# Expert tiles without a bias product: the bias as the 128th weight row, and first-layer weights copied from SBUF

## The chip, the cores and the metric

The program runs on one core of a Trainium2 chip. Its time is the device time in microseconds (us) of one execution; the kernel before has a median of 607.71 us over three runs. Engines are named as the profile names them: PE (TensorE, its matmuls), PEld (its weight loads), DVE (VectorE), ACT (ScalarE), POOL (GpSimd) and SP (SyncE, which only issues transfers here). SPq and ACTq are the transfer instructions on SP and ACT. Sixteen DMA engines carry all transfers, whoever issues them.

## The reference, cut to what matters

Four sequences of 512 tokens of 128 numbers go through attention (16 heads), an expert layer, a scan layer, and the same expert layer again, each on a layer norm of its input and added to it:

```python
x = x + attn_a(layernorm(x)); x = x + ffn(layernorm(x)); x = x + attn_b(layernorm(x)); x = x + ffn(layernorm(x))

def ffn(xf):                       # xf [2048, 128]; 8 experts, each token goes to the 2 with the highest scores
    scores = sigmoid(xf @ Wg.T + bg + bias)
    top_scores, top_idx = top_k(scores, 2)
    h = gelu(einsum('td,ehd->teh', xf, W1) + b1)        # W1 [8, 512, 128], b1 [8, 512]
    eo = einsum('teh,edh->ted', h, W2) + b2
    combined = einsum('ted,te->td', eo, weights)
    shared = gelu(xf @ Ws1.T + bs1) @ Ws2.T + bs2       # a ninth, shared expert for all tokens
    return shared + combined
```

`layernorm` has no scale or shift, so the 128 numbers of a token that enters `ffn` add up to zero.

## The kernel before

It is written engine by engine: each engine runs a fixed list of instructions, and semaphores hold them together. What comes in which order is written out by hand, in tables (`TOPS_TO`, `PIECES_TO`, `SLOTS_IN`, `Q_IN` and others) that hang small steps on the 32 steps of the attention loop, and in `bank_order`, which says who gets a PSUM bank next.

**Attention** (about 30 to 220 us). One step n of the loop is one pair of heads of one sequence a = n // 8. For step n PE makes the scores of pair n + 2, DVE takes their row maxima, PE turns the maxima (`turn_max`), ACT copies them (`copy_max`), SP places them as two more rows of the queries (`place_max(n)`, two transfers of 2 x 4 x 128 numbers, line 623, 8 pieces of 256 bytes each), and then PE makes the transposed scores of pair n (`scores_T`, line 1340) for the exponentials on ACT. `scores_T(n, 0)` waits for `place_max(n)`. The queries and keys of sequences 1 to 3 are rotated by POOL (`rope(a)`, lines 768 to 777) one sequence ahead, and placed by SP (`place_some`, line 603). Of sequence 0, ACT places three parts itself (line 948, 128 rows each). Ahead of the loop SP loads the small constants of the scan layer, `a_mat` and `wdt` among them (128 rows each).

**Loads of the expert weights.** ACT issues eight loads (`ffn_loads`, line 1020) at about 24 to 27 us: `wg`, `gate_rows` (2 rows), the first-layer weights of all nine experts as `w1_raw` [128, 4608] float32, `b1`, the second-layer weights `w2_raw` of the same size, `b2` (9 rows), `grids` and `counts`; all but the two named have 128 rows, one to a partition. SP also uses the time of the attention for `fill`: transfers that set the row lists in DRAM to empty rows, 512 pieces of 520 bytes each, two after most steps from n = 2 on (line 628). DVE finds the largest weight (`find_tops`, 16 pieces in steps 2 to 13), and in steps 17 to 31 ACT and DVE split each weight into two float16 numbers, high and low (`take_high_weights`, `take_low_weights`). SP then stores the split `w1` to DRAM (`weights_dram`, line 652).

**Expert tiles.** Each expert layer r sorts the tokens into lists in DRAM (`scatter`, POOL, 32 transfers) and then runs over NT = 39 tiles of up to 128 tokens of one expert. DVE works out which expert and which rows each tile has (`map_tiles`). For a tile SP loads its first-layer weights from `weights_dram` (128 rows of 2 KB, line 679, eight tiles ahead) and its token rows (line 687). PE turns the token rows (line 1600), makes `up`, which is one bias product of 96 x 128 by 96 x 512 numbers (line 1606) and twelve products of 128 x 128 (line 1612), and `down` for the tile three back (lines 1626 and 1627). ACT applies gelu (line 1155) and makes the high part of the hidden numbers (line 1160), DVE the low part (line 2135), DVE adds up the result (line 2143), and POOL sends it to DRAM (line 884). The bias product takes 96 rows `bias_rows`, which POOL makes from `b1` after the attention (`bias_table`, lines 840 to 849), and a table `which`, which `map_tiles` makes (line 2098, four instructions).

## Time and profile before

| | |
|---|---|
| median of three runs | 607.71 us (602.28 to 608.34) |
| the profiled execution | 606.08 us |
| its span, first to last instruction | 604.2 us |
| granted PE clock, mean over the span | 0.942 |
| PE busy | 501.5 us (83%) |
| DVE busy | 432.9 us (72%) |
| ACT busy | 331.9 us (55%) |
| POOL busy | 265.1 us (44%) |

The span is about 2 us shorter than the profiled execution's own time. Busy shares are averages over stages that differ much; the two tile stages are about 297 to 372 us and 507 to 584 us of the span, the attention ends at about 220 us. All times from the trace are counted from the start of the span.

### The profile page before, as it was taken

What the parts mean: (1) busy time and instruction counts of PE and PEld (TensorE: products, weight loads), DVE (VectorE), ACT (ScalarE), POOL (GpSimd) and SP (SyncE); (2) the same over time, 40 slices, a digit from 0 to 9 for tenths busy, and PEclk for the clock granted to TensorE, in tenths of its full rate; (3) what the DMA queues carried; (4) which work ended last, traced back from release to release, by engine and by line L of the source; (5) the groups of instructions that cost most, each with busy time, mean ns of one, the idle gap of its engine ahead of it and who ended that gap; (6) DMA issues with size and microseconds to landing.
All of it is one profiled execution on the core that took longest, in us unless ns stands there. A gap on an engine that the chain in (4) does not pass through costs nothing.

```text
span 604.2 us, 14288 instructions
## 1 busy us (share of the span) xinstructions
PE 501.5 (83%) x5019; PEld 320.3 (53%) x5021; DVE 432.9 (72%) x1162; ACT 331.9 (55%) x509; POOL 265.1 (44%) x247
## 2 busy tenths in 40 slices
PE   7778879878888888679999987879989977989950
PEld 2335556545656545334688775224545544878730
DVE  5658897686787968566377874798789663767745
ACT  1337556654777652546377863246657833757730
POOL 5509550045000037777046555373256770555550
PEclk9999999996999988888999999869999998999985
DMA  4863533441421370111588651997000016777516
GB/s 119 221 254 108 143 108 90 113 120 47 129 60 55 109 240 1 40 50 45 154 233 235 200 179 41 258 195 110 10 28 28 31 50 179 220 215 208 168 42 208
DMA packets 85708, 76.14 MB, mean 126 GB/s; under 512 B 9645, under 2 KB 72614, under 8 KB 85382
## 3 DMA queue, kind: packets, MB, share of 16 engines
q1 hardware_dynamic: 76320, 57.86, 36.6%
q0 software_dynamic: 4544, 9.38, 4.5%
q10 hardware_dynamic: 4774, 7.98, 3.7%
q8 instruction: 42, 0.69, 0.5%
q14 instruction: 28, 0.23, 0.1%
HBM read 37.88 MB, written 30.88 MB: 114 GB/s over the span
## 4 chain that ended last, share of the span: by engine, by line
PE 27%; DVE 9%; issue 5%; ACT 5%; another core or an unknown queue 4%; DMA 3%; POOL 1%; SPq 1%; ACTq 0%; DVEq 0%; POOLq 0%
PE ps L1612 6%; PE ps L1626 4%; PE ps L1627 3%; PE ps L1483 3%; DMA arena<-y_dram 2%; PE ps L1606 2%; DVE probs L2135 2%; ACT arena L1155 1%; PE ps L1560 1%; PE ps L1538 1%; DVE x_all L2164 1%; PE ps L1698 1%; DVE x_all L2160 1%; PE ps L1600 1%
## 5 line engine op out<-in xcount | busy, mean ns | idle before, releaser
L884 POOL DMA_INDIRECT y_dram<-arena,goes_to x78 | 85.0, 1090 | 90.5 <-DVE goes_to L2123 65.7
L1874 DVE TENSOR_REDUCE max_words<-ps 128x2 f32<-128x256 f32 (+3 forms) x128 | 98.0, 817 | 24.4 <-PE ps L1316 24.2
L955 ACT ACTIVATE probs<-ps 128x768 f32<-128x768 f32 (+1 forms) x96 | 81.1, 885 | 50.0 <-PE ps L1345 49.8
L730 POOL TENSOR_TENSOR rstd<-var_eps,minus_half 128x4 f32<-128x4 f32 x16 | 17.5, 1094 | 147.5 <-DVE var_eps L1841 147.5
L1155 ACT ACTIVATE arena<-ps,up_back 128x512 f32<-128x512 f32 x78 | 53.0, 680 | 52.1 <-PE ps L1612 28.6
L875 POOL DMA_INDIRECT rows_dram<-probs,idx x64 | 68.5, 1071 | 25.6 <-issue 18.6
L1626 PE MATMUL ps<-w,probs 128*128 x312 | 60.5, 273 | 11.7 <-DVE probs L2135 10.9
L1612 PE MATMUL ps<-arena 128*128 128x128 f16 x936 | 64.9, 219 | 4.0 <-DVE arena L2129 3.7
L2135 DVE SCALAR_TENSOR_TENSOR probs<-arena,hid_scale,probs 128x512 f16<-128x512 f32 x78 | 58.4, 748 | 11.5 <-ACT probs L1160 5.7
L1612 PEld LDWEIGHTS ps<-arena 128*128 128x128 f16 x936 | 57.8, 97 | 16.2 <-issue 8.7
L1483 PE MATMUL ps<-w,ident_f 128*128 128x512 f16 x184 | 56.3, 428 | 11.5 <-ACT arena L1111 3.3
L1160 ACT ACTIVATE probs<-arena,hid_scale 128x512 f16<-128x512 f32 x78 | 56.3, 722 | 2.6
L1627 PE MATMUL ps<-w,probs 128*128 x312 | 56.0, 219 | 0.6 <-issue 0.6
L2143 DVE TENSOR_REDUCE arena<-ps 128x128 f32<-128x256 f32 x78 | 32.9, 421 | 28.8 <-PE ps L1627 20.8
L1340 PE MATMUL ps<-heads_arena 64*128 64x512 bf16 (+3 forms) x256 | 38.2, 312 | 14.3 <-ACT probs L955 7.5
L1311 PE MATMUL ps<-heads_arena 62*128 62x128 bf16 (+3 forms) x256 | 36.5, 305 | 9.8 <-DVE max_words L1874 8.2
L1365 PE MATMUL ps<-probs,v_tok 128*32 128x256 f32 (+3 forms) x512 | 42.8, 452 | 2.0 <-ACT probs L955 2.0
L1626 PEld LDWEIGHTS ps<-w,probs 128*128 128x128 f16 x312 | 30.5, 98 | 18.6 <-issue 15.1
L1483 PEld LDWEIGHTS ps<-w,ident_f 128*128 128x128 f16 x184 | 18.0, 107 | 36.0 <-issue 13.7
L1316 PE MATMUL ps<-mask_qk,neg_eye 64*128 64x128 bf16 x512 | 34.3, 218 | 0.0
L1345 PE MATMUL ps<-mask_kq,neg_eye 64*128 64x128 bf16 x512 | 32.3, 221 | 0.0
L1627 PEld LDWEIGHTS ps<-w,probs 128*128 128x128 f16 x312 | 30.5, 98 | 1.1 <-issue 1.0
(242 smaller groups left out, 1033.7 us busy)
## 6 DMA issues: line engine op xcount, KB each, us to landing
arena<-weights_dram SPq DMA_DIRECT2D x78, 256.0 KB
rows_dram<-grids SPq DMA_DIRECT2D x64, 260.0 KB, 4.0
heads_arena<-q_words SPq DMA_DIRECT2D x45, 128.0 KB, 2.4
qk_sb<-rows_dram SPq DMA_DIRECT2D x78, 65.0 KB
arena<-in_w ACTq DMA_DIRECT2D x2, 2304.0 KB
weights_dram<-w SPq DMA_DIRECT2D x2, 1152.0 KB, 8.0
arena<-y_dram SPq DMA_DIRECT2D x16, 128.0 KB, 5.2
arena<-y_dram ACTq DMA_DIRECT2D x16, 128.0 KB, 5.3
```

The source lines that it names most:

```text
L875: nc.gpsimd.indirect_dma_start(rows_dram[r].ap(), bass.IndirectOffsetOnAxis(ap=idx[:, r, b, t, k:k + 1], axis=0), xrow_words_of(r, b)[:, t ...
L884: nc.gpsimd.indirect_dma_start(y_dram.ap(), bass.IndirectOffsetOnAxis(ap=goes_to[:, n % AT_GO:n % AT_GO + 1], axis=0), y_t[:, n % YT, :], ...
L955: nc.scalar.activation(probs[:, n % 2, :, PROB_AT[u]:PROB_AT[u] + size], ps[:, of:of + 2, 0:size], ACT.Exp).then_inc(slot_free[slot_of(("T ...
L1155: nc.scalar.activation(hid_t[:, n % HT, :], ps[:, of, :], ACT.Gelu, scale=up_back[:]).then_inc(bank_free[of], 1)
L1160: nc.scalar.activation(hid16_t[:, n % HT, 0, :], hid_t[:, n % HT, :], ACT.Identity, scale=hid_scale[:]).then_inc(high_t_ready, 1)
L1365: mm = pe.matmul(ps[group:group + OW, PV_BANK, j * P:L], v_flat[:, at_v:at_v + OW], probs[:, n % 2, h, at[j]:at[j] + L - P * j], start=(p ...
L1483: pe.matmul(ps[:, to, :], ident_f16[:], w1[:, 0, 0, :], start=True, stop=True, skip_group_check=True)
L1612: mm = pe.matmul(ps[:, to, c * P:(c + 1) * P], w1t[:, s % WT, w, c * P:(c + 1) * P], xgT[:, n % GT, v, :], start=False, stop=(v == 1), ski ...
L1626: pe.matmul(halves, hid16_t[:, n % HT, 0, c * P:(c + 1) * P], parts, start=(c == 0), stop=False, skip_group_check=True)
L1627: mm = pe.matmul(halves[:, 0, :], hid16_t[:, n % HT, 1, c * P:(c + 1) * P], parts[:, 0, :], start=False, stop=(c == C - 1), skip_group_che ...
L1874: ins = nc.vector.tensor_reduce(max_words[:, n % 2, :, t], ps[:, of:of + 2, o:o + keys], AX.X, ALU.max)
L2135: nc.vector.scalar_tensor_tensor(hid16_t[:, n % HT, 1, :], hid_t[:, n % HT, :], hid_scale[:], hid16_t[:, n % HT, 0, :], ALU.mult, ALU.subt ...
```

## The change

The tokens of an expert tile add up to zero over their 128 numbers, so the last weight row can be taken off all others: the sum over 128 numbers of w[d] x[d] is the sum over 127 of (w[d] - w[127]) x[d]. The change does that for the eight listed experts, and uses the freed 128th row for the bias: the 128th number of each token row is a constant (`X_SCALE`, low part 0), and the 128th weight row is `b1`. The shared expert keeps its weights. In parts:

1. `up` loses its bias product; `bias_rows`, `bias_table`, `which` and `weight_row` go, and with them the load `b1e`.
2. The last weight row, repeated for 127 partitions (`last_w1`, [127, 4096] float32, 16 KB a partition), is loaded by a ninth transfer on ACT's queue, into the memory that the split `w1` takes later. POOL waits for it and for the eight others, and takes it off `w1_raw` in two instructions, between `rope(1)` and `add_bias(2)`.
3. `find_tops` takes the second-layer weights first (steps 2 to 8) and the first-layer weights after that, once POOL is done (`less_last`). Pieces are now 9 x 512 numbers for each layer, not 8 x 576.
4. POOL writes the constants into the token rows (`set_constants`, two small memsets, twice), and the token rows are split 127 numbers wide.
5. The split `w1` lies in SBUF expert by expert ([128, 9, 2, 512]), and SP loads a tile's weights from there, 2 KB from each partition to the same partition. The store to DRAM goes, and the wait for it.

```diff
-TOPS_TO = [0, 0, 0, 1, 2, 4, 5, 6, 8, 9, 10, 12, 13, 14] + [16] * (PAIRS - 13)
+TOPS_TO = [0, 0, 0, 1, 2, 4, 5, 7, 8, 10, 11, 13, 15, 16] + [18] * (PAIRS - 13)
...
-        w1 = sb("w1", [P, 2, X, F], F16)
+        w1_sb = sb("w1", [P, X, 2, F], F16)
+        w1 = w1_sb[:].rearrange("p x w f -> p w x f")
...
+        last_w1 = w1_sb[:].rearrange("p e w f -> p (e w f)").bitcast(F32)[0:D - 1, 0:E * F]
...
             sp.wait_ge(low_ready, PIECES)
-            for w in range(2):
-                sp.dma_start(of_parts[:, w], w1[:, w]).then_inc(weights_stored, 16)
...
-                    sp.dma_start(wt[:, s % WT, :], weights_dram.ap()[bass.ds(weights_at[s], P), :]).then_inc(wt_loaded[s % WT], 16)
+                    sp.dma_start(wt[:, s % WT, :], w1_sb[:, bass.ds(weights_at[s], 1), :, :].rearrange("p o w f -> p (o w f)")).then_inc(wt_loaded[s % WT], 16)
...
             rope(1)
+            pool.wait_ge(ffn_in, 16 * len(ffn_loads))
+            pool.wait_ge(last_w1_loaded, 16)
+            for half in range(2):
+                of = slice(half * E * F // 2, (half + 1) * E * F // 2)
+                raw = arena[0:D - 1, of]
+                nc.gpsimd.tensor_tensor(raw, raw, last_w1[:, of], ALU.subtract).then_inc(less_last, 1)
             add_bias(2)
...
+            def set_constants(rows):
+                nc.gpsimd.memset(rows[:, :, :, D - 1], X_SCALE)
+                link(nc.gpsimd.memset(rows[:, :, :, 2 * D - 1], 0.0))
...
-                high, low = (xrow_of(r, b)[:, :, k * D:(k + 1) * D] for k in range(2))
-                link(nc.gpsimd.tensor_copy(high, xf_of(r, b)))
-                nc.gpsimd.tensor_tensor(low, xf_of(r, b), high, ALU.subtract).then_inc(rows_ready, 1)
+                if g == 0:
+                    set_constants(xrow4)
+                high, low = (xrow_of(r, b)[:, :, k * D:(k + 1) * D - 1] for k in range(2))
+                tokens = xf_of(r, b)[:, :, 0:D - 1]
+                link(nc.gpsimd.tensor_copy(high, tokens))
+                nc.gpsimd.tensor_tensor(low, tokens, high, ALU.subtract).then_inc(rows_ready, 1)
...
             for dst, src in ffn_loads:
                 nc.scalar.dma_start(whole(dst), src).then_inc(ffn_in, 16)
+            nc.scalar.dma_start(last_w1, last_w1_in).then_inc(last_w1_loaded, 16)
...
-                    pe.matmul(ps[:, to, :], bias_rows[0:BIAS_ROWS, :], which[0:BIAS_ROWS, s, :].unsqueeze(2).broadcast_to([BIAS_ROWS, C, P]),
-                              start=True, stop=False, skip_group_check=True)
...
             def find_tops(k, piece):
...
+                if k == 0:
+                    dve.wait_ge(less_last, 1 if (piece + 1) * PIECE <= E * F // 2 else 2)
...
-                for c in range(C):
-                    nc.vector.tensor_scalar(which[:, :, c], expert_of[:], grids[:, MOD_AT + c:MOD_AT + c + 1], None, ALU.is_equal)
                 nc.vector.tensor_copy(tile_expert[:], expert_of[:])
-                nc.vector.tensor_scalar(weight_row[:], expert_of[:], float(P), None, ALU.mult)
...
-        "b1e": np.tile(a["L0_ffn_b1"].reshape(E * C, P), (3, 1)),
+        "last_w1": np.repeat(w1[0:E, :, D - 1].reshape(1, E * F), D - 1, 0),
```

ACT's instructions near 24 to 31 us, before the change; `in_w` are the two weight loads, `b` is `b1` and then `b2`, and behind the loads stand the copy of the turned tokens of sequence 1 and the first copy of maxima:

```order
L971 ACTIVATE xn<-x_all,shift,rstd 128x128 x4
L1020 DMA wg<-in_wg 128x8
L1020 DMA gate_rows<-in_gate_rows 2x32
L1020 DMA arena<-in_w 128x4608
L1020 DMA b<-in_b 128x36
L1020 DMA arena<-in_w 128x4608
L1020 DMA b<-in_b 9x128
L1020 DMA grids<-in_grids 128x293
L1020 DMA counts<-in_counts 128x256
L964 COPY xnT<-ps 128x512
L978 COPY max_rows<-ps 16x128
```

The same place after it:

```order
L957 ACTIVATE xn<-x_all,shift,rstd 128x128 x4
L1006 DMA wg<-in_wg 128x8
L1006 DMA gate_rows<-in_gate_rows 2x32
L1006 DMA arena<-in_w 128x4608
L1006 DMA b<-in_b 128x36
L1006 DMA arena<-in_w 128x4608
L1006 DMA b<-in_b 9x128
L1006 DMA grids<-in_grids 128x286
L1006 DMA counts<-in_counts 128x256
L1007 DMA w<-in_last_w 127x4096
L950 COPY xnT<-ps 128x512
L964 COPY max_rows<-ps 16x128
```

The new transfer of 127 rows stands last on ACT's queue, behind the eight others and ahead of nothing but compute.

POOL's instructions from the end of `rope(1)` to the start of `rope(2)`, before:

```order
L772 CAST q_words<-rope_c 128x1024
L774 TENSOR_TENSOR rope_s<-rope_c,q_words 128x1024
L775 CAST q_words<-rope_s 128x1024
L777 TENSOR_TENSOR q_words<-rope_s,q_words 128x1024
L750 TENSOR_TENSOR x_all<-x_all,bo 128x512
L768 TENSOR_TENSOR rope_c<-q_words,k_words 128x1024
L769 TENSOR_TENSOR rope_s<-q_words,k_words 128x1024
```

And after:

```order
L761 CAST q_words<-rope_c 128x1024
L763 TENSOR_TENSOR rope_s<-rope_c,q_words 128x1024
L764 CAST q_words<-rope_s 128x1024
L766 TENSOR_TENSOR q_words<-rope_s,q_words 128x1024
L790 TENSOR_TENSOR arena<-arena,w 127x2048 x2
L739 TENSOR_TENSOR x_all<-x_all,bo 128x512
L757 TENSOR_TENSOR rope_c<-q_words,k_words 128x1024
L758 TENSOR_TENSOR rope_s<-q_words,k_words 128x1024
```

The two subtractions, each 127 x 2048 numbers (`arena` is `w1_raw`, `w` is `last_w1`), stand ahead of `add_bias(2)` and of all of `rope(2)`, and so does POOL's wait for the new transfer.

PE in the middle of a tile stage, one tile's last `down` products, its turned tokens and its `up`, before:

```order
L1626 ISA
L1626 MATMUL ps<-w,probs 128x256
L1627 MATMUL ps<-w,probs 128x128
L1600 MATMUL ps<-ident_f,qk_sb 128x128 x2
L1606 MATMUL ps<-weighed,bias_rows 128x512
L1612 MATMUL ps<-arena 128x128 x12
L1626 ISA
L1626 MATMUL ps<-w,probs 128x256
```

And after:

```order
L1610 ISA
L1610 MATMUL ps<-w,probs 128x256
L1611 MATMUL ps<-w,probs 128x128
L1586 MATMUL ps<-ident_f,qk_sb 128x128 x2
L1596 MATMUL ps<-arena 128x128 x12
L1610 ISA
L1610 MATMUL ps<-w,probs 128x256
```

The product of 128 x 512 numbers between the turned tokens and the twelve `up` products is gone; nothing else moves.

## Rows read from the trace of the kernel before

**Rows 1.** the page, part 1: busy us (share), instructions
```profile
PE 501.5 (83%) x5019; PEld 320.3 (53%) x5021; DVE 432.9 (72%) x1162; ACT 331.9 (55%) x509; POOL 265.1 (44%) x247
```

**Rows 2.** windows: busy us (count) PE, PEld, DVE, ACT, POOL; PEclk, DMA share, GB/s
```profile
300.00:317.00 17.00, 16.00 (x217) 13.76 (x216) 12.50 (x35) 12.48 (x20) 7.29 (x7) 1.00 0.79 227
297.00:372.00 75.00, 67.53 (x891) 57.28 (x889) 54.55 (x154) 53.04 (x78) 39.41 (x37) 1.00 0.63 185
```

**Rows 3.** timeline of PE in the first tile stage: start us, duration us
```profile
337.35 0.38 PE L1606 MATMUL ps<-weighed,bias_rows 96*128 96x512 bf16 x1
337.57 0.83 PE L1612 MATMUL ps<-arena 128*128 128x128 f16 x12
339.01 0.38 PE L1606 MATMUL ps<-weighed,bias_rows 96*128 96x512 bf16 x1
```

**Rows 4.** line L1606 in either tile stage: min/median/max ns, first and last start
```profile
L1606 PE MATMUL ps<-weighed,bias_rows x39: 381/381/382, 297.4 to 367.5; 96*128 96x512 bf16 x39
...
L1606 PE MATMUL ps<-weighed,bias_rows x39: 381/381/464, 507.0 to 577.9; 96*128 96x512 bf16 x39
```

**Rows 5.** timeline of ACT in the first tile stage, after a gap
```profile
327.53 0.67 ACT L1155 ACTIVATE arena<-ps,up_back 128x512 f32<-128x512 f32 x1
328.86 0.67 ACT L1155 ACTIVATE arena<-ps,up_back 128x512 f32<-128x512 f32 x1
```

**Rows 6.** waits of ACT in either tile stage: us, times, longest
```profile
ACT arena L1155 <- remote: 8.4, 4, 2.2
...
ACT arena L1155 <- remote: 13.3, 7, 3.2
```

**Rows 7.** timeline of DVE at the end of the second tile map
```profile
496.43 0.71 DVE L2098 TENSOR_SCALAR weighed<-weighed,grids 128x39 bf16<-128x39 f32 x4
```

**Rows 8.** timeline of POOL ahead of the first scatter
```profile
239.03 1.03 POOL L730 TENSOR_TENSOR rstd<-var_eps,minus_half 128x4 f32<-128x4 f32 x1 [1.90 <-DVE var_eps L1841]
```

**Rows 9.** DMA view, 20 to 80 us: GB/s per 1.5 us, queue, issues (KB, us to landing)
```profile
GB/s 206 291 204 234 415 404 392 381 407 395 394 394 335 36 2 5 14 174 181 0 0 26 291 52 8 160 197 222 124 100 169 179 260 73 286 4 14 235 120 0
...
q10 hardware_dynamic: 1318, 5.36, 23.7%
...
gate_rows<-in_gate_rows ACTq DMA_DIRECT2D x1, 0.2 KB
a_mat<-in_a_mat SPq DMA_DIRECT2D x1, 16.0 KB, 4.5
wdt<-in_wdt SPq DMA_DIRECT2D x1, 1.0 KB, 10.1
...
b<-in_b ACTq DMA_DIRECT2D x1, 4.5 KB
```

**Rows 10.** timeline of PE: transposed scores of pairs 0, 3 and 4
```profile
40.27 0.39 PE L1340 MATMUL ps<-heads_arena 64*128 64x512 bf16 x2 [1.76 <-DMA heads_arena<-max_rows]
...
56.14 0.39 PE L1340 MATMUL ps<-heads_arena 64*128 64x512 bf16 x2
...
62.22 0.39 PE L1340 MATMUL ps<-heads_arena 64*128 64x512 bf16 x2
```

**Rows 11.** timeline of SP: fills after pair 2, maxima of pair 3, fills after it
```profile
44.83 1.77 SPq L628 DMA_DIRECT2D rows_dram<-grids  x2
50.80 1.07 SPq L623 DMA_DIRECT2D heads_arena<-max_rows  x2
51.91 0.95 SPq L628 DMA_DIRECT2D rows_dram<-grids  x2
```

**Rows 12.** timeline of POOL between the rotations of sequences 1 and 2
```profile
60.64 1.27 POOL L750 TENSOR_TENSOR x_all<-x_all,bo 128x512 f32<-128x512 f32 x1
68.45 2.35 POOL L768 TENSOR_TENSOR rope_c<-q_words,k_words 128x1024 f32<-128x1024 f32 x1 [6.53 <-ACT q_words L991]
...
80.04 2.13 POOL L777 TENSOR_TENSOR q_words<-rope_s,q_words 128x1024 bf16<-128x1024 f32 x1
```

**Rows 13.** timeline of ACT: norm of sequence 3 applied
```profile
96.65 1.65 ACT L971 ACTIVATE xn<-x_all,shift,rstd 128x128 f32<-128x128 f32 x4
```

More of the change, by code:

```diff
@@ L56 @@
 Q = 4
-PIECES = 8
-PIECE = X * F // PIECES
+PIECES = X
+PIECE = F
+TOPS_OF = [(k, piece) for k in (1, 0) for piece in range(PIECES)]
 PRODUCTS = [(0, 0), (1, 0), (0, 1)]
```

72 lines of the change are left out of this document (20 added, 52 removed).

## The prediction

> **What bounds the kernel now.** I read the page first: PE is busy 83% of the span, more than any other engine [rows 1], but that is an average. The windows of the first tile stage show PE at 67.5 of 75 us, DVE at 54.6, ACT at 53.0, with the clock granted in full and the DMA engines busy 0.63 of the time [rows 2]. So PE leads there, and the timeline says by how much: from one bias product to the next it is 339.01 - 337.35 = 1.66 us, which is PE's own list of work for one tile without a gap [rows 3]. When ACT has fallen behind and catches up, it starts a gelu every 328.86 - 327.53 = 1.33 us [rows 5]. That is how fast ACT can go; PE can't go below 1.66. Over 39 tiles the mean is longer, (367.5 - 297.4) / 38 = 1.84 us in the first stage and 70.9 / 38 = 1.87 us in the second [rows 4]: 7.0 and 7.8 us beyond 38 x 1.66 = 63.1 are gaps. In the view of waits ACT stood 8.4 and 13.3 us for something that the profile has no name for [rows 6].
>
> The attention is another matter. Its loop is a ring: maxima on DVE, a copy on ACT, a tiny transfer by SP, and only then PE's transposed scores. What holds up SP's tiny transfer holds up everything.
>
> **The bias product.** It costs PE 337.57 - 337.35 = 0.22 us a tile [rows 3], so PE's tile goes from 1.66 to 1.44 us, still above ACT's 1.33. The most this can give is 38 x 0.22 = 8.4 us a stage, 16.7 in all. It won't be all of it: after a gap ACT gains on PE 0.33 us a tile now and only 0.11 then, so a gap of 2.1 us (8.4 / 4) is made up in 20 tiles and not in 6, and more of each reaches the end. If every one of ACT's waits of that kind came on top of PE's work, the stages would take 54.7 + 8.4 = 63.1 and 54.7 + 13.3 = 68.0 us, 7.0 and 2.9 less than now. Between 9.9 and 16.7 I take 11.3, near the low end, because the gaps come every five to ten tiles.
>
> **The map.** Four instructions, 0.71 us together [rows 7], end some 10 us ahead of the first tile of the second stage at 507.0 [rows 4], and SP's reads and loads for that tile wait for them: 0.7 us. In the first stage PE still has other work when the map is done, so nothing. Gains so far: 12 us, between 10 and 18.
>
> **What I cost at nothing.** POOL's bias table goes, but right behind it POOL waits 1.90 us for DVE before the norm's root and the first scatter [rows 8]: DVE sets that point, not POOL, and the small memsets fit into the same hole. The store of the split weights has no reader until the tiles. The copies 127 wide have the same instruction count, 0 to 1 us. The pieces of the weights are 18 for 16 and of 512 numbers for 576, the same sum, 0 to 1 us. The copy from SBUF moves the same bytes in the same 128 pieces; at 1.44 us a tile the DMA share of 0.79 [rows 2] would be 0.79 x 1.66 / 1.44 = 0.91, tight but below 1, and loads are asked for eight tiles ahead. No row has this copy; if it were slower by a tenth the engines would be full and the gain of the tiles would shrink to about 5 us, if it is quicker nothing is gained, since PE doesn't wait for weights.
>
> **The new load.** This is the term that decides. It is 127 rows of 16,384 bytes, 2.08 MB. How many of the 16 DMA engines take it? The trace lets one count. ACT's queue shows 1318 packets between 20 and 80 us [rows 9]. The rows of its transfers are 3 x 128 (placements), 128 (`wg`), 2 (`gate_rows`), 2 x 128 (the weights), 128, 9, 128 and 128, together 1163. The other 155 are the signals that each engine sends when its share is done: nine transfers of 128 rows make 9 x 16 = 144, and 11 are left for the transfers of 2 and of 9 rows. So these two ran on 2 and 9 engines, and every transfer I can count is cut into equal shares. 127 is a prime: in equal shares it goes to one engine. The other reading, one row after another dealt to up to 16 engines, also gives 2 and 9; no row has a count above 16 that isn't a multiple of 16. I take equal shares, with 0.85, since no transfer here is seen cut unequally.
>
> The Trainium skill, "DMA: Bandwidth & Descriptors", section on why a DMA increments its semaphore by 16, says that the engines used are the largest number up to 16 that divides the outer sizes of both sides, and that 127 partitions go to one engine. The counts of 2 and 9 agree with it; no run here shows 127. By it the single engine would be certain, and the sum the same.
>
> While the two big loads ran, the eight full slices of 1.5 us moved 381 to 415 GB/s, 398 in the mean [rows 9]; that is 24.9 GB/s for one engine, 0.66 us for a row of 16 KB and 84 us for 127. The engine is free for it at about 40.5 us, where the slices fall off. It ends at 124.5 us.
>
> Meanwhile it takes turns with SP's transfers on that engine, piece by piece. `wdt`, 1 KB in 128 pieces, eight to an engine, took 10.1 us to land beside the big loads, `a_mat`, 16 KB and as many pieces but issued ahead of them, 4.5 [rows 9]: 5.6 us for about eight turns, 0.7 each. And pair 0 waited for its maxima, which were behind these [rows 10]. Now count the pieces on that engine. A fill has 512, 32 to an engine and a signal. The two fills issued at 44.83 [rows 11] are 66 turns, 44 us; the maxima of pair 3, issued at 50.80 behind them, 10 more turns (two transfers on 2 engines, 4 pieces and a signal each), 7 us. So pair 3 starts at about 95 us, not 56 [rows 10]. Of the 66 turns of the next two fills [rows 11] some 44 fit in before 124.5; then the queue runs free, and the maxima of pair 4, behind them, land at about 127. Pair 4 starts 65 us late (62.2 before, rows 10), and nothing behind it makes that up, as PE's list lets the scores run only two pairs ahead.
>
> **POOL's part.** A subtraction of 1024 numbers takes 2.35 us [rows 12] (the same instruction on 128 x 1024), so 4 x 2.35 = 9.4 us for 2 x 2048. It waits until 124.5, so `rope(2)` starts at 124.5 + 9.4 + 1.3 = 135.2 instead of 68.45 and ends 13.7 us later, at 149. ACT's next use, the norm of sequence 3, was at 96.65 [rows 13] and is now at 162: covered by the 65 us themselves. The two delays don't add up.
>
> **Sum**, against the profiled execution: 606.1 - 12 + 65 = 659. The median of the runs is 1.6 above it: 660.
>
> **Rivals.** (A) The load goes over all 16 engines. Then 2.08 MB at 398 GB/s is 5 us, it lands at 46, before POOL is through with `rope(1)` at 60.6 [rows 12]. The subtraction uses POOL's idle 6.5 us and makes `rope(2)` 2.9 us late, against a slack of 14 us to row 96.65 [rows 13]. What is left is the gain: 607.7 - 12 = 596, faster. It decides by one thing, the engines that take 127 rows. Chance 0.13.
>
> (B) One engine, but SP's pieces aren't held back much. Against it stands `wdt`; for it, that those turns were with 18 KB rows on all engines at once. Then POOL's chain decides: `rope(2)` and the root behind it are through at about 150, the norm at 96.65 moves to 150, 54 us late. 607.7 - 12 + 54 = 650. The Trainium skill, same page, section on queues, rings and completion order, says that an engine drains a whole packet, typically 9 to 17 descriptors, from one ring before it turns to the next; that would let the 66 pieces through in some five turns, and would give this case. The 10.1 us of `wdt` speak for single turns. Chance 0.12.
>
> Forecast 0.73, anything else 0.02.
>
> **Range.** The forecast's own: a row at 0.69 us makes 88 us and 69 late, with a gain of 10 that is 667; PE's clock may fall while it stands and cost a few more; with 80 us of load and a gain of 16 it is 650. (B) reaches down to 643. 640 to 676 holds both, 0.8 in all; (A) is left out. A measurement of this kernel tells about 1% (6 us) from no change. Faster 0.13, same 0.01, slower 0.86.
>
> **What the profile after would show.** Right: a stretch of some 80 us from 40 us on with the DMA share near 1/16 and about 25 GB/s; transposed scores of pair 3 near 95 and of pair 4 near 127 us, ended by the maxima's transfer; POOL idle until 124 with the load as releaser; tile stages of 63 to 66 us, PE's tile 1.44. Wrong: the load landed before 60 us (A); pairs 3 to 8 in step and a stand at pair 8 or 9 (B); tiles at 1.66 or waits for `wt_loaded`, then the copy from SBUF is the limit.

## The result

The changed kernel took 674.96 us in the median of four runs (671.82 to 678.62); the kernel before, beside it, 605.22 (602.28 to 608.34, four runs). The ratio is 1.1154, 95% interval 1.1053 to 1.1254: slower, by 70 us. The profiled execution took 671.8 us with a span of 669.9, against 606.1 and 604.2 before. Here and below a ratio compares only the runs that lie within 1.5% of the fastest of their kernel, so it can be lower than the quotient of the medians, most of all in e7 (5 of 8 runs, 0.979 where the medians give 0.986), e8 (2 of 6, 1.019 and 1.030) and e11 (4 of 9, 0.983 and 0.994).

The page of the changed kernel, part 1, two lines of part 4 and a group of part 5:

```profile
PE 493.9 (74%) x4943; PEld 321.0 (48%) x4943; DVE 433.8 (65%) x1156; ACT 333.2 (50%) x511; POOL 267.8 (40%) x242
...
PE 38%; DVE 26%; DMA 8%; SPq 7%; ACT 7%; issue 7%; another core or an unknown queue 4%; POOL 1%; DVEq 0%; ACTq 0%; POOLq 0%
DVE max_words L1858 7%; PE ps L1596 6%; SPq L618 6%; DMA heads_arena<-max_rows 5%; PE ps L1610 4%; PE ps L1470 3%; PE ps L1362 3%; PE ps L1611 2%; PE ps L1352 2%; PE ps L1278 2%; ACT probs L941 2%; DMA arena<-y_dram 1%; PE ps L1327 1%; DVE w L1913 1%
...
L1327 PE MATMUL ps<-heads_arena 64*128 64x512 bf16 (+3 forms) x256 | 39.1, 318 | 70.1 <-DMA heads_arena<-max_rows 58.8
```

PE does 7.6 us less work than before [rows 1] and the span is 65.7 us longer, so the time went into a wait. The last line names it: the transposed scores stood 58.8 us for the tiny transfer of the maxima. SP's issue of it (line 618) and that transfer hold 6% and 5% of the chain.

The DMA view of 50 to 100 us (GB/s in slices of 1.25 us), and the issue of the fills in it:

```profile
GB/s 26 27 26 27 28 234 220 40 34 27 27 27 27 27 27 27 27 27 27 27 27 14 27 27 27 27 27 27 27 27 27 27 27 27 27 27 26 27 26 27
...
rows_dram<-grids SPq DMA_DIRECT2D x2, 260.0 KB, 35.1
```

A steady 27 GB/s is one engine of sixteen. The trace holds the new load as 127 packets of 16,384 bytes, one behind another, the first at 39.9 and the last at 119.8 us, 0.62 us each and one every 0.63. Of the two fills issued in this stretch, at 55.60 and 56.05, the profile has 4.0 and 66.2 us to landing; 35.1 is the middle of the two. The packet records (queue, start and size of each) show what holds them up. Behind every row of 16,384 bytes on ACT's queue stands one piece of SP's queue, then comes the next row. From 54.1 us on these are 32 pieces of 520 bytes and a signal of 4 bytes, twice (the fills issued at 45.0; second signal at 95.17), and then four pieces of 256 bytes and a signal, twice (the maxima of pair 3; second signal at 101.36): 76 turns in 47 us. The records name no engine, and up to 59.8 us pieces of other engines stand among them; from there on it is exactly one piece of SP's to a row. Timelines of PE (scores of pairs 3 and 4; 56.14 and 62.22 before, rows 10), SP and POOL:

```profile
101.80 0.61 PE L1327 MATMUL ps<-heads_arena 64*128 64x512 bf16 x2 [41.43 <-DMA heads_arena<-max_rows]
123.22 0.61 PE L1327 MATMUL ps<-heads_arena 64*128 64x512 bf16 x2 [12.92 <-DMA heads_arena<-max_rows]
```

```profile
45.02 0.96 SPq L623 DMA_DIRECT2D rows_dram<-grids  x2
54.49 1.06 SPq L618 DMA_DIRECT2D heads_arena<-max_rows  x2
55.60 0.95 SPq L623 DMA_DIRECT2D rows_dram<-grids  x2
59.62 39.76 SPq L618 DMA_DIRECT2D heads_arena<-max_rows  x1
```

```profile
121.62 8.98 POOL L790 TENSOR_TENSOR arena<-arena,w 127x2048 f32<-127x2048 f32 x2 [60.88 <-DMA w<-in_last_w]
...
132.70 2.35 POOL L757 TENSOR_TENSOR rope_c<-q_words,k_words 128x1024 f32<-128x1024 f32 x1 [0.88 <-ACT q_words L977]
```

Two fills go out at 45.02 as they did before [rows 11], the maxima of pair 3 behind them at 54.49, and these arrive only for 101.80. SP's next issue even takes 39.76 us by itself: by the look of it, and not shown, no further piece fits behind what already waits on that engine. POOL stands 60.88 us for the load.

The first row of products of the tiles (line 1596, before 1612) in either stage, with min/median/max ns, then first and last start; the first two lines are the kernel before:

```profile
L1612 PE MATMUL ps<-arena x468: 216/219/219, 297.9 to 368.4; 128*128 128x128 f16 x156
...
L1612 PE MATMUL ps<-arena x468: 216/219/220, 507.5 to 579.9; 128*128 128x128 f16 x156
```

```profile
L1596 PE MATMUL ps<-arena x468: 216/220/312, 361.5 to 435.0; 128*128 128x128 f16 x156
...
L1596 PE MATMUL ps<-arena x468: 216/220/315, 569.3 to 646.1; 128*128 128x128 f16 x156
```

I call the distance between these two starts the length of a stage. It was 70.5 and 72.4 us and is 73.5 and 76.8: **longer**, not shorter. Yet PE's tile is as short as forecast (371.37 to 372.81, 1.44 us). The timeline of PE in the changed kernel, two tiles without a gap and then the largest gap, at tile 29:

```profile
371.37 0.83 PE L1596 MATMUL ps<-arena 128*128 128x128 f16 x12
372.81 0.83 PE L1596 MATMUL ps<-arena 128*128 128x128 f16 x12
...
411.11 0.83 PE L1596 MATMUL ps<-arena 128*128 128x128 f16 x12 [1.05 <-issue]
415.75 0.39 PE L1610 MATMUL ps<-w,probs 128*128 x1 [3.80 <-issue]
...
417.21 1.49 PE L1596 MATMUL ps<-arena 128*128 128x128 f16 x12
```

Behind the gap the same twelve products take 1.49 us instead of 0.83: the granted clock has fallen from 2.4 to 1.2 GHz while PE stood. Its mean over the stages is 0.98 and 0.96; before it was 1.00 in both.

The books of the two spans: the first stage starts 63.6 us late (361.5 to 297.9), it is 3.0 longer, the stretch between the stages is 4.8 shorter (134.3 to 139.1), the second stage 4.4 longer, the end 0.5 shorter (669.9 - 646.1 to 604.2 - 579.9). Sum 65.7. The stretch between the stages goes with the clock more than with the edit: the granted clock in it was 0.91 before and 0.94 after; e1 has 0.94 and 135.0 us, e2 and e3 0.91 and 139.8 and 138.8. What set the clock there isn't shown.

### The profile page after: what moved, and what is told of

Its sections match the earlier page's. It is cut to its first block, busy times and chain, and to the rows that moved or that the text cites. A ratio compares the mean times of both kernels' runs of the same rounds, so it can differ in the third digit from the quotient of the medians.

```text
span 669.9 us, 14041 instructions
## 1 busy us (share of the span) xinstructions
PE 493.9 (74%) x4943; PEld 321.0 (48%) x4943; DVE 433.8 (65%) x1156; ACT 333.2 (50%) x511; POOL 267.8 (40%) x242
## 4 chain that ended last, share of the span: by engine, by line
PE 38%; DVE 26%; DMA 8%; SPq 7%; ACT 7%; issue 7%; another core or an unknown queue 4%; POOL 1%; DVEq 0%; ACTq 0%; POOLq 0%
DVE max_words L1858 7%; PE ps L1596 6%; SPq L618 6%; DMA heads_arena<-max_rows 5%; PE ps L1610 4%; PE ps L1470 3%; PE ps L1362 3%; PE ps L1611 2%; PE ps L1352 2%; PE ps L1278 2%; ACT probs L941 2%; DMA arena<-y_dram 1%; PE ps L1327 1%; DVE w L1913 1%
## 5 line engine op out<-in xcount | busy, mean ns | idle before, releaser
L1327 PE MATMUL ps<-heads_arena 64*128 64x512 bf16 (+3 forms) x256 | 39.1, 318 | 70.1 <-DMA heads_arena<-max_rows 58.8
L1596 PE MATMUL ps<-arena 128*128 128x128 f16 x936 | 67.0, 224 | 16.5 <-DVE arena L2112 12.2
L1610 PE MATMUL ps<-w,probs 128*128 x312 | 62.5, 280 | 17.1 <-issue 10.5
L1470 PE MATMUL ps<-w,ident_f 128*128 128x512 f16 x184 | 53.8, 411 | 10.3 <-ACT arena L1098 3.5
L1611 PE MATMUL ps<-w,probs 128*128 x312 | 57.7, 223 | 0.0
L1147 ACT ACTIVATE probs<-arena,hid_scale 128x512 f16<-128x512 f32 x78 | 56.3, 722 | 2.5
L1327 PEld LDWEIGHTS ps<-heads_arena 64*128 64x128 bf16 x256 | 12.9, 96 | 83.3 <-issue 63.9
L1298 PE MATMUL ps<-heads_arena 62*128 62x128 bf16 (+3 forms) x256 | 38.0, 316 | 9.3 <-DVE max_words L1858 7.3
L1610 PEld LDWEIGHTS ps<-w,probs 128*128 128x128 f16 x312 | 31.1, 100 | 24.1 <-issue 19.0
L790 POOL TENSOR_TENSOR arena<-arena,w 127x2048 f32<-127x2048 f32 x2 | 9.0, 4512 | 60.9 <-DMA w<-in_last_w 60.9
```

Source lines behind the costliest of these rows:

```text
L1147: nc.scalar.activation(hid16_t[:, n % HT, 0, :], hid_t[:, n % HT, :], ACT.Identity, scale=hid_scale[:]).then_inc(high_t_ready, 1)
L1327: pe.matmul(ps[:, to + h, o:o + size], kT[rows, a % 2, p, j * P:(j + 1) * P], q1T[rows, a % 2, p, j * P:L], start=True, stop=False)
L1470: pe.matmul(ps[:, to, :], ident_f16[:], w1[:, 0, 0, :], start=True, stop=True, skip_group_check=True)
L1596: mm = pe.matmul(ps[:, to, c * P:(c + 1) * P], w1t[:, s % WT, w, c * P:(c + 1) * P], xgT[:, n % GT, v, :], start=((w, v) == (0, 0)), stop= ...
L1610: pe.matmul(halves, hid16_t[:, n % HT, 0, c * P:(c + 1) * P], parts, start=(c == 0), stop=False, skip_group_check=True)
L1611: mm = pe.matmul(halves[:, 0, :], hid16_t[:, n % HT, 1, c * P:(c + 1) * P], parts[:, 0, :], start=False, stop=(c == C - 1), skip_group_che ...
```

## The experiments

Twelve kernels ran, e1 to e4, e5 to e8 and e9 to e12 on one chip each. The kernel before, run beside them, took 607.4, 583.6 and 584.3 us. So the ratios count, and absolute times are compared within four only; what the first chip has that the others haven't comes under 4. No trace of the kernel before was kept from the second and third chip; on the third e9 and e10, which have its tiles, stand in for it. A stage length comes from one execution of each kernel, in e7 the slowest of eight. All results, with the lengths of the two stages in the profiled execution:

| kernel | copies from | product | lists | ratio | stages, us |
|---|---|---|---|---|---|
| before | DRAM | 96 rows | before's | | 70.5, 72.4 |
| changed | SBUF | none | moved | 1.1154 | 73.5, 76.8 |
| e1, 128 rows | SBUF | none | moved | 1.0152 | 73.7, 74.7 |
| e2 | DRAM | none | before's | 1.0002 | 68.6, 70.4 |
| e3 | SBUF | 12 rows, zeros | moved | 1.0216 | 76.9, 79.2 |
| e4, before + load | DRAM | 96 rows | before's | 1.1042 | 71.4, 70.2 |
| e5 | SBUF | none | experts' moved back | 1.0075 | 64.6, 63.1 |
| e6 | DRAM | none | aligned | 0.9735 | 56.3, 58.7 |
| e7, before | DRAM | none | before's | 0.9792 | 59.2, 61.4 |
| e8 | SBUF | 96 rows, zeros | moved | 1.0193 | 74.0, 72.2 |
| e9, e4 + late fills | DRAM | 96 rows | before's | 1.0878 | 63.4, 63.6 |
| e10, before | DRAM | 96 rows | aligned | 0.9987 | 63.7, 65.2 |
| e11, as e2 | DRAM | none | before's | 0.9827 | 59.2, 60.0 |
| e12 | SBUF | none | aligned | 0.9860 | 60.0, 62.4 |

**1. The number of rows (e1).** The changed kernel with a load of 128 rows:

```diff
-        last_w1 = w1_sb[:].rearrange("p e w f -> p (e w f)").bitcast(F32)[0:D - 1, 0:E * F]
+        last_w1 = w1_sb[:].rearrange("p e w f -> p (e w f)").bitcast(F32)[:, 0:E * F]
-                nc.gpsimd.tensor_tensor(raw, raw, last_w1[:, of], ALU.subtract).then_inc(less_last, 1)
+                nc.gpsimd.tensor_tensor(raw, raw, last_w1[0:D - 1, of], ALU.subtract).then_inc(less_last, 1)
-        "last_w1": np.repeat(w1[0:E, :, D - 1].reshape(1, E * F), D - 1, 0),
+        "last_w1": np.repeat(w1[0:E, :, D - 1].reshape(1, E * F), D, 0),
```

> The changed kernel with one thing altered: the input and the load of the last weight row are 128 rows instead of 127 (16 KB more to move); POOL still subtracts on 127 partitions. One-engine theory (the 127 rows lie on one DMA engine because 127 has no divisor up to 16 but 1, and SP's pieces take turns with them there): the load is cut over 16 engines and lands before about 48 us, pair 3 starts at about 56 us and pair 4 at about 62, as in the kernel before, and the first tile stage starts at about 298 us, 63.6 earlier than in the changed kernel. The time then is 671.8 - 63.6 = 608 for the profiled execution if the tile stages stay as long as in the changed kernel (72.9 and 76.2 us from the first row of products to the last), and 596 if they have the length that my prediction gave them (63 to 66 us each). Rival (the bytes or POOL's subtraction hold up the ring, not the number of rows): 655 to 672, pair 3 at about 100 us.

616.3 us, ratio 1.0152 (1.009 to 1.0215). One row more is 59 us less. The 128 packets now start between 38.7 and 44.7 us, still 0.61 us each: the same work on sixteen engines. Timelines of POOL and of PE (pair 3):

```profile
60.12 9.04 POOL L790 TENSOR_TENSOR arena<-arena,w 127x2048 f32<-127x2048 f32 x2
...
70.35 2.34 POOL L757 TENSOR_TENSOR rope_c<-q_words,k_words 128x1024 f32<-128x1024 f32 x1
```

```profile
56.01 0.39 PE L1327 MATMUL ps<-heads_arena 64*128 64x512 bf16 x2
```

POOL's subtraction lies where I put it for this case (rival A), and makes the rotation 1.9 us late. But the total is 20 us above the 596 of that rival: its stages are 73.7 and 74.7 us long. And its first stage starts at 308.5 us where I expected 298. That isn't the load's: e3, with the same attention on the same chip, starts it at 299.4. The granted clock up to that point was 0.92 in e1, 0.95 in e3 and 0.95 before, so some 9 us of e1's lateness goes with the clock of the one execution that was traced. The load is settled by this run and the next; the tiles are not.

**2. The load alone (e4).** The kernel before with the 127-row load, and with no one who reads it:

```diff
...
+            nc.scalar.dma_start(last_w1, last_w1_in).then_inc(last_w1_loaded, 16)
...
                     act.wait_ge(scales_ready, 1)
+                    act.wait_ge(last_w1_loaded, 16)
```

> The kernel before with the 127-row load alone added, behind ACT's other loads as in the changed kernel, into the memory of the split weights. Nothing reads it; only ACT's first instruction that writes this memory (pair 17, at about 145 us before) waits for it. Turn-taking theory (SP's fills and the maxima behind them take turns piece by piece with the rows on that engine): the load stands on one engine from 40 to 120 us, pair 3 at about 100 and pair 4 at about 123 us, total 606 + 62 to 66 = 668 to 672. Rival B of the prediction (SP isn't held, POOL's subtraction behind the load was what held up the ring): pairs 3 and 4 at 56 and 62 us, total 605 to 610.

669.8 us, ratio 1.1042 (1.0957 to 1.1127), 62 us slower, pairs 3 and 4 at 101.3 and 122.5. So POOL's chain isn't needed for the loss, and rival B falls.

**3. The fills out of the way (e9).** The same with

```diff
-FILLS_FROM = 2
+FILLS_FROM = 12
...
-                    for r, i, start, rows in fills[filled_to:filled_to + (1 if n in SLOTS_IN else 2)]:
+                    for r, i, start, rows in fills[filled_to:filled_to + (1 if n in SLOTS_IN else 3)]:
```

> The kernel before with the 127-row load that nobody reads, as in the run of the load alone, and SP's fills moved behind it: none from pair 2 to pair 11, three a pair from pair 12 on. Turn-taking theory: what held pairs 3 and 4 were the 66 pieces of two fills on the loaded engine ahead of each pair's maxima; without them only the maxima (about 10 turns a pair of 0.61 us, 6 us) and the placings of pairs 4 and 5 take turns there, so no pair stands for 40 us; pair 3 starts at 57 to 63 us, pair 5 at 75 to 95, and the kernel is 10 to 35 us slower than before instead of 62. Rival (any transfer of SP's queue that touches the engine waits for the whole load): pair 3 at about 120 us, 60 us slower whatever the fills do.

633.6 us against 584.3, ratio 1.0878 (1.0819 to 1.0937): 51 us slower, a miss above my range. Timeline of SP, line 605 the placings of keys and queries, 625 the maxima:

```profile
60.48 3.80 SPq L605 DMA_DIRECT2D heads_arena<-q_words  x6
73.58 1.14 SPq L625 DMA_DIRECT2D heads_arena<-max_rows  x2
74.82 22.58 SPq L605 DMA_DIRECT2D heads_arena<-q_words  x6
97.45 30.26 SPq L625 DMA_DIRECT2D heads_arena<-max_rows  x4
```

Pair 3 starts at 66.0 and pair 4 at 74.3, so the rival (about 120 for pair 3) is out and without fills the ring keeps going, each pair some turns late. What I had under-counted are the placings: 128 pieces each, 8 on that engine and a signal, nine turns. The six issued from 60.48 on are 54 turns; in the packet records their pieces of 1,024 bytes take the gaps between the rows from 72.1 to 108.5 us. The maxima of pair 5, issued at 73.58 behind them, take the next ten, to 114.7, and pair 5 starts at 115.3. The last four of the other six placings take 4.85, 5.57, 5.57 and 5.19 us to issue (most of the 22.58 above), about what nine turns of 0.62 last, 5.6. So without fills too SP's pieces take turns with the rows one for one.

**4. The tiles: source, product, halts (e2, e3, e7, e8, e11).** First the copies from DRAM again, without the product:

```diff
+            sp.dma_start(weights_dram.ap().rearrange("(x p) (w f) -> p x w f", p=P, w=2), w1_sb[:]).then_inc(weights_stored, 16)
...
-                    sp.dma_start(wt[:, s % WT, :], w1_sb[:, bass.ds(weights_at[s], 1), :, :].rearrange("p o w f -> p (o w f)")).then_inc(wt_loaded[s % WT], 16)
+                    sp.dma_start(wt[:, s % WT, :], weights_dram.ap()[bass.ds(weights_at[s], P), :]).then_inc(wt_loaded[s % WT], 16)
```

> The 128-row kernel with one thing put back as before: the split weights are stored to DRAM after the attention and the tiles' copies come from there (with the map's multiplication that this needs). No product with the bias. Theory S (the tile stages of the changed kernel are long because the copies from SBUF disturb other transfers): stages of 63 to 66 us, total 10 to 16 us below the 128-row kernel with SBUF copies. Theory P (the stages are bounded by something that does not care how short PE's list is, or PE's clock falls when its list is shorter): stages of 71 to 76 us, total within 3 us of the 128-row kernel with SBUF copies, 605 to 612.

607.4 us, ratio 1.0002 (0.9955 to 1.005), stages 68.6 and 70.4 us. Both theories miss: the source, with what hangs on it, is worth 5.1 and 4.3 us a stage against e1, but the stages don't come near 63 to 66, only 1.9 and 2.0 below the kernel before. Then a product of zeros with copies from SBUF, 12 rows high and 96 rows high:

```diff
+                    pe.matmul(ps[:, to, :], zeros[0:12, :], zeros[0:12, 0:C].unsqueeze(2).broadcast_to([12, C, P]),
+                              start=True, stop=False, skip_group_check=True)
```

> The 128-row kernel with a product put back at the place of the bias product, of the same shape (12 rows, 4 x 128 columns) and of zeros, so that the result stays the same; the copies still come from SBUF. PE's tile is 1.66 us again. Theory S: the stages are as long as in the 128-row kernel or longer, 73 to 80 us, total 608 to 618. Theory P with the clock (a shorter list lets the clock fall to half for 3.4 us at a time): the clock stays at full, stages of 70 to 72 us as before, total 603 to 608. My prediction's own arithmetic: 12 us slower than the 128-row kernel.

> The run with the product put back, with the product now 96 rows high as the bias product is, instead of 12 (the zeros of 12 rows took 0.42 us of PE's tile, the bias product 0.22). Copies from SBUF, list at the changed kernel's place. Height theory: PE's tile is 1.66 us, stages of 73 to 76 us, total 612 to 618. Rival (what makes the tile 1.87 us there is something else, such as the operand that is read over and over): tile 1.87, stages 77 and 79 us, total 617 to 621.

e3: ratio 1.0216 (1.0167 to 1.0265), stages 76.9 and 79.2; e8: 1.0193 (1.0098 to 1.0289), 74.0 and 72.2. They ran on different chips. The timelines of PE, e3 first, show that the stand-in of e3 was no fair one:

```profile
329.73 0.38 PE L1594 MATMUL ps<-zeros 12*128 12x512 bf16 x1
330.05 0.84 PE L1600 MATMUL ps<-arena 128*128 128x128 f16 x12
```

```profile
330.04 0.38 PE L1594 MATMUL ps<-zeros 96*128 96x512 bf16 x1
330.25 0.83 PE L1600 MATMUL ps<-arena 128*128 128x128 f16 x12
```

The next product starts 0.32 us behind the 12-row one and 0.21 behind the 96-row one; the turned tokens before them start 0.21 and 0.12 us ahead of them, and the tiles are 1.86 and 1.66 us. The height theory holds in the tile; of the 3 and 7 us between the stages of e3 and e8 I make nothing, since the chips differ too. The product alone, taken out of the kernel before (the next product then has `start=((w, v) == (0, 0))`):

```diff
-                    pe.matmul(ps[:, to, :], bias_rows[0:BIAS_ROWS, :], which[0:BIAS_ROWS, s, :].unsqueeze(2).broadcast_to([BIAS_ROWS, C, P]),
-                              start=True, stop=False, skip_group_check=True)
```

> The kernel before with the bias product alone left out: PE's first product of a tile overwrites instead of adding, everything else, the bias table too, stays. The first layer of the listed tiles is computed without its bias. Its tile on PE is 1.44 us. My prediction's gain for this alone: 10.6 us (9.9 to 16.7 with nothing for the map), total 591 to 597. Theory from the 128-row kernel with copies from DRAM (the short halts of all engines every five or six tiles cost what they last, and PE can no longer work through them): stages of 68.6 and 70.3 us instead of 70.4 and 72.4, total 602 to 604.

575.3 us against 583.6 in the medians, 8 us; ratio 0.9792 (0.974 to 0.9843), which is 12 us (9 to 15). Either is nearer to my forecast's gain of 10.6 than to the theory from the first chip. So e2 was run again:

> The 128-row kernel with copies from DRAM once more, beside the others of this call. On the chip of the first call all engines stood still for a moment every five or six tiles in both stages, and this kernel was as fast as the one before (1.0002). On a chip without such halts, as in the second call, the kernel before without the product was 2.1% faster. If the halts ate the product's gain: ratio 0.980 to 0.988 where the traces show no halts, 0.997 to 1.003 where they do. Rival (POOL's subtraction, the wider load and the copies eat it): ratio near 1.000 on either chip.

580.6 us against 584.3 in the medians (0.994), ratio 0.9827 (0.9781 to 0.9873), stages of 59.2 and 60.0 us: the same kernel whose ratio was 1.0002 on the first chip. So the gain is 1.7% by the ratio and 0.6% by the medians; on the first chip it is nothing by either. The waits of both in the first stage, e2 (304 to 374 us) and e11 (301 to 360):

```profile
ACT arena L1146 <- remote: 10.7, 5, 2.2
DVE arena L2131 <- remote: 7.4, 5, 2.0
```

```profile
ACT arena L1146 <- PE ps L1600: 7.0, 4, 2.9
DVE arena L2131 <- PE ps L1615: 3.9, 3, 2.9
```

In e2 ACT and DVE each stand five times for something that the profile has no name for ("remote"); e11 has no such wait. The traces of e1, e2 and e4 have four to seven such waits of ACT in each tile stage, as those of the kernels before [rows 6] and after; e3, with the longest tile on PE, has one, of DVE, in its first stage and four in all in its second; none of e5 to e12 has one there. In the changed kernel (timeline of ACT) one reads

```profile
379.99 0.69 ACT L1142 ACTIVATE arena<-ps,up_back 128x512 f32<-128x512 f32 x1 [2.32 <-remote]
```

Without the halts PE's tiles follow each other at their own pace for a dozen and more in a row. On the chip with them the stages of this kernel are 9.4 and 10.4 us longer (e2 against e11). Those of the kernel with the product are only 8.0 and 6.6 us longer (e4 against e9, which have the same tiles). So what the product's absence gives in the two stages is 7.8 us on the chip without halts (e9 to e11) and 2.6 on the chip with them (e4 to e2). That halts hit the shorter list harder fits this. It is argued from two chips and not shown, for nothing here could switch the halts off, and what causes them stays open.

**5. The list of experts (e5, e6, e10, e12).** PE reads the expert of each tile from SBUF into registers, 13 at a time, the last 13 in the middle of a stage, at tile 29. These reads, in the changed kernel and in the kernel before (min/median/max ns, first and last start):

```profile
L1565 PEldq TENSOR_LOAD <-weighed x6: 1105/3810/4608, 344.2 to 622.5; - x6
```

```profile
L1578 PEldq TENSOR_LOAD <-weighed x6: 1207/3118/3407, 282.5 to 559.6; - x6
```

The two reads in mid-stage took 4.22 and 4.49 us in the changed kernel and 1.28 and 1.21 before: this is the gap of 3.80 us above, and the change as printed doesn't show where it comes from. With the list of multiplied numbers gone, `tile_expert` moved from place 6 to place 5 of its area, and its last third begins at byte 884 instead of 1040. e5 moves it back:

```diff
-        tile_row, tile_expert = (weighed[:, NT * i:NT * (i + 1)].bitcast(I32) for i in range(4, 6))
+        tile_row, tile_expert = (weighed[:, NT * i:NT * (i + 1)].bitcast(I32) for i in (4, 6))
```

> The 128-row kernel with copies from SBUF, and the tiles' list of experts moved back by 39 words to the place that it has in the kernel before (SBUF words 234 to 272 of the area instead of 195 to 233); nothing else. PE reads the last 13 of its numbers in the middle of a stage, at tile 29. Alignment theory: that read took 1.1 to 1.3 us where its first number lay on a multiple of 16 bytes (byte 1040, kernel before) and 4.0 to 5.2 us where it did not (byte 884), so the gap at tile 29 falls from 4.6 to 5.1 us to about 2, each stage gets 3 us shorter (70.7 and 71.7 us from the first row of products to the last), and the time is 616.3 - 6 = 610. Rival (the copies from SBUF slow the read, wherever the list lies): the gap stays, total 614 to 618.

587.6 us against 583.6, ratio 1.0075 (1.0036 to 1.0114), where e1 was at 1.0152. The read at tile 29 takes 1.44 and 1.67 us; in e8, on the same chip and with copies from SBUF too but the list at the changed kernel's place, it takes 4.80 and 4.64. The rival falls; how much of the rest is the other chip's can't be told. Then all lists of the DRAM variant on multiples of 16 bytes:

```diff
-GROUPS = (0, 4, 13, 26, NT)
-EXPERTS = (0, 13, 26, NT)
+GROUPS = (0, 4, 12, 24, NT)
+EXPERTS = (0, 12, 24, NT)
-        tile_row, weight_row, tile_expert = (weighed[:, NT * i:NT * (i + 1)].bitcast(I32) for i in range(4, 7))
+        tile_row, weight_row, tile_expert = (weighed[:, 40 * i:40 * i + NT].bitcast(I32) for i in range(4, 7))
```

> The 128-row kernel with copies from DRAM, and every list that SP and PE read into registers laid on multiples of 16 bytes: the three lists start every 40 words instead of every 39, and are read in groups of 4, 8, 12 and 15 numbers (SP) and 12, 12 and 15 (PE), instead of 4, 9, 13 and 13, and 13, 13 and 13. Alignment theory: all of SP's reads take 0.3 to 0.9 us (now up to 2.9), PE's two reads ahead of the tiles 1.1 us each and not 3.1, which lie on the path ahead of the second stage: 3 to 4 us there, 0 to 2 in the stages, total 601 to 604. Rival (reads are as long as they are by the number of numbers, or none of them ends on the path): 605 to 609.

569.6 us against 583.6, ratio 0.9735 (0.9686 to 0.9783): the fastest of all, stages 56.3 and 58.7. The reads of SP and of PE, e11 (lists as before) and e6:

```profile
L658 SPq TENSOR_LOAD <-weighed x16: 322/1555/3147, 283.8 to 526.9; - x16
```

```profile
L1569 PEldq TENSOR_LOAD <-weighed x6: 1113/3156/3474, 286.6 to 536.6; - x6
```

```profile
L658 SPq TENSOR_LOAD <-weighed x16: 307/714/1633, 282.7 to 517.0; - x16
```

```profile
L1569 PEldq TENSOR_LOAD <-weighed x6: 850/976/1772, 285.4 to 526.2; - x6
```

Sorted by place they are plain: SP's 4, 8 and 12 numbers from a multiple of 16 bytes take 0.31, 0.52 and 0.75 us and its 15 numbers 1.5, while 9 and 13 from elsewhere take 1.87 and 2.8 to 3.1, some 0.21 a number. The size of the group isn't the cause: in e11 already, where some groups happen to begin on such a multiple, 9 numbers take 0.77 us there and 13 take 0.98. The Trainium skill, "Runtime: NRT & Kernel Launch", section on instruction fetch mechanics, gives about 200 ns a register even in bulk, for loads from HBM. The unaligned reads here, which are from SBUF, come to as much; the aligned ones of up to 13 numbers are some three times quicker. The same in the kernel before:

> The kernel before with its three lists laid on multiples of 16 bytes and read in groups that begin on such multiples, as in the aligned run; the bias product, the store and everything else as before. Alignment theory: PE's two reads ahead of each tile stage take 0.9 us each instead of 3.1 to 3.4, two of them on the path ahead of the second stage (5 to 6 us), and SP's later ones in a stage 0.8 to 1.6 instead of 2.8; 6 to 11 us faster than before, ratio 0.982 to 0.990. Rival (the 15.5 us of the aligned run were the product's, the alignment hides): ratio 0.997 to 1.003.

583.3 us, ratio 0.9987 (0.9955 to 1.0018): nothing. My expectation misses, and its rival holds in the ratio, though the reads did get short. Once the product is gone the same edit takes the ratio from 0.9827 (e11) to 0.9735 (e6), some 5 us, on two chips and with intervals that just touch; the stages are 2.9 and 1.3 us shorter. I read it so: at 1.66 us a tile SP has time for its slow reads, at 1.44 it hasn't. In the first stage of e9, with the product, SP's issue of a tile's weights starts at least 5.7 us ahead of the tile; in e11, with the same reads, only 3.0 at the lowest, behind the last two reads, and there PE's tiles follow at 3.6, 2.4 and 2.1 us. The profile names nothing that PE waited for there, so this is argued and not shown. Last, the aligned lists with copies from SBUF (the two lists at places of 40 words):

> The 128-row kernel with copies from SBUF and the two lists that it has aligned and read in groups as in the aligned run. It differs from that one (ratio 0.9735) only in where the copies come from. If the place of the list was all that made the copies from SBUF look slow: the same ratio within 0.005. If the source costs time of its own (SP's issue of such a copy takes 0.49 us instead of 0.33, and every read of a list is 0.3 to 0.8 us longer beside such copies): ratio 0.980 to 0.992.

577.6 us, ratio 0.986 (0.981 to 0.9911), stages 60.0 and 62.4, so the source has a price of its own, some 7 us (3 to 11, from two chips). SP's timeline, e12 and then e11, where it waits for nothing:

```profile
321.37 0.49 SPq L670 DMA_DIRECT2D arena<-w  x1
322.10 0.40 SPq L678 DMA_DIRECT2D qk_sb<-rows_dram  x1
322.66 0.49 SPq L670 DMA_DIRECT2D arena<-w  x1
```

```profile
323.82 0.33 SPq L673 DMA_DIRECT2D arena<-weights_dram  x1
324.39 0.33 SPq L681 DMA_DIRECT2D qk_sb<-rows_dram  x1
324.90 0.33 SPq L673 DMA_DIRECT2D arena<-weights_dram  x1
```

A tile costs SP 322.66 - 321.37 = 1.29 us with copies from SBUF and 1.08 from DRAM. The packets themselves aren't slower (2048 bytes: 0.09 us in the mean from SBUF, 0.11 from DRAM). PE's tile is 1.44, so SP gains 0.15 or 0.36 us a tile, and each later pair of list reads costs it 1.7 to 3.7 us in e12 and 4.0 to 5.9 in e11. In the first stage of e12 the issue of a tile's weights ends 6.2 us ahead of their use at tile 10 and only 1.9 at tile 24; about there PE's tiles follow at 2.8, 2.6 and 3.4 us instead of 1.44. In e6 it is never less than 5.9 in that stage, though 3.3 in the second.

## Why the prediction was right, and where it wasn't

**The load** was right in mechanism and size. One engine took all 127 rows (e1 against the changed kernel), at 0.63 us a row where I took 0.66, so it ended at 120 and not at 124.5. Pair 3 came at 101.8 where I had 95: I let the fills' turns begin at 44.8, but pair 2's maxima, 10 turns issued at 43.95, stood ahead and freed pair 2 only at 54.7; from there 66 and 10 turns of 0.63 us give 102. Pair 4 came at 123.2 where I had 127, and the attention ends 64 us late where the sum had 65. The load alone made 62 (e4). Rival A's condition is false by the trace, rival B's by e4.

Single turns are shown by the packet records: one piece of SP's behind each row from 54.1 to 101.4 us. The Trainium skill, "DMA: Bandwidth & Descriptors", section on queues, rings and completion order, says that an engine drains a packet of typically 9 to 17 descriptors before it switches; here it switched after every one. In the prediction I took that rule to favour B, which was wrong: ACT's rows would go 9 to 17 at a turn as well, and by my estimate five turns of that many rows, at 0.63 us a row, are 28 to 54 us, which would have held pair 3 up much as single turns do. So `wdt`, the late pairs and the slow issues of e9 don't tell the two apart; the packets do. The Trainium skill, same page, section on why a DMA increments its semaphore by 16, says one engine for 127 partitions, and the trace agrees: 127 rows one behind another.

PE's clock, for which the range kept a few us, did fall: its mean was 0.55 from 60 to 101 us, while PE stood (1.00 before), and pair 3's first products took 0.61 us instead of 0.39.

**POOL's part**: forecast 9.4 us from 124.5, a rotation at 135.2; measured 8.98 from 121.62 and 132.70. Covered by the late ring, as said.

**The tiles** are the step that failed: "Between 9.9 and 16.7 I take 11.3". The stages became 7.4 us longer. Three things are in it, in the traces of the first chip: the shorter list gave 3.9 (e2 against before), the copies from SBUF with their list took 9.4 (e1 against e2), and 1.9 are left over that no pair of runs assigns. Single traces repeat such sums to 1 us or so: the tiles of the kernel before took 142.9 us and in e4 141.6. Of the 9.4 PE's read at tile 29 is 6.1 (3.96 and 4.32 us in e1, 1.11 and 1.10 in e2), and most of the rest is the clock that falls behind it: from tile 28's first product to tile 30's, read and slow products together, e1 takes 7.90 and 8.04 us and e2 3.54 and 3.72, which is 8.7 of the 9.4. So in the stages of that chip it was the moved list that cost, and the copies little beside it. My lower bound of 9.9 added ACT's unnamed waits as they were before, 8.4 and 13.3 us, to 54.7. In e2 they are 10.7 and 15.5, and its stages are 54.7 + 13.9 and 54.7 + 15.7. So the waits were longer with the shorter list, and the bound was none. Why they were is argued only: halts come every five or six tiles, and both ACT (1.33) and SP (1.08 to 1.29 and the reads) have too little left to PE's 1.44. On the chips without halts the product is worth 12 us by e7's ratio (9 to 15) and 8 by its medians; 9.9 to 16.7 fits the one and not the other.

**Cost at nothing** was wrong for "the copy from SBUF": I looked at bytes and engines, not at SP, whose issue went from 0.33 to 0.49 us; and the place of a list in memory, the larger of the two on the first chip, wasn't in my parts at all. The map's 0.7 us can't be told apart in the 4.8 us by which the stretch between the stages is shorter; PE's two reads in it went from 3.12 and 3.12 to 4.61 and 1.10, 0.5 us less together, and the rest goes with the clock, as said above.

**Sum**: forecast 606.1 - 12 + 65 = 659; measured 606.1 + 65.7 = 671.8 in the profiled execution. The miss is 65.7 - 53 = 12.7 us and no single term: the stages came out 18.7 us worse than forecast (7.4 longer where I had 11.3 off), the load 1.4 better (63.6 for 65), and the stretch between the stages and the end 5.3 shorter where I had 0.7 for the map. The median, 675.0, was 3 us above that execution and 1 below the top of my range. That the range held is in part luck: its upper part was made for slower rows and a gain of 10, and the rows were quicker and the gain a loss.

## What to carry to other kernels

Count the rows of a transfer and factor them: 127 rows of 16 KB stood on one engine for 80 us, and 128 took 6 on sixteen. A slow transfer on one engine held every small one that was cut over all of them, one row of its own for each of their pieces, so look for what is queued there, not for who reads the load. When an engine's list gets shorter, add up the queue that feeds it, register reads included: with 128 rows and copies from DRAM the gain was 1.7% (0.6% in the medians) with lists where they were, and 2.65% (2.4%) with lists on multiples of 16 bytes. And when an edit takes a list out of memory, see which other list moves. The version to keep has 128 rows, copies from DRAM and aligned lists. It ran on one chip without halts; on the chip with them it is untested.

## What the hardware showed unasked

- A register list that starts on a multiple of 16 bytes was read by SP in 0.31 us for four numbers and about 0.22 per further four up to 12 (15 took 1.5); elsewhere in 0.21 us per number. Beside copies from SBUF SP's reads within a stage took 0.05 to 1.0 us more (e1 against e2, e12 against e6), those of 8 and 9 numbers ahead of it the same; PE's 13 unaligned numbers ahead of the second stage took 4.4 to 4.7 us (e1, e3, e5, e8) instead of 3.1 to 3.4 (e2, e4, e7, e9, e11).
- A product 12 rows high between products 128 rows high cost 0.42 us a tile, one 96 rows high 0.22, at the same 0.38 us of its own.
- SP's issue of a copy from SBUF at an address in a register took 0.49 us, from DRAM 0.33.
- In the tile stages ACT and DVE stood for nothing that the profile names, up to 3.6 us at a time and mostly every five or six tiles, on one chip and never on two others; the same kernel (e2, e11) took 607 us there and 581 here.
- Two queues on one DMA engine, rows of 16,384 bytes on the one and pieces of 256 to 1,024 bytes on the other, alternated one for one for 47 us (e4 and e9 show it too).
